# Carrying each token's row number through the experts: scattered results and plain loads in an eight-stage block

## The reference

```
# stage 1: 8 experts, each token goes to the best one, weighted by its probability
x = x + tanh(g_ffn[0]) * p[e*] * (w2[e*] gelu(w1[e*] ln(x) + b1[e*]) + b2[e*])

# stage 3: 8 experts of width 352, each token goes to the best two, beside a shared expert
logits = ln(x) @ gate_w.T ; topk_w, topk_i = top_k(softmax(logits), 2)
eo  = w_down[e] (silu(w_gate[e] ln(x)) * (w_up[e] ln(x)))
out = sum over the two of topk_w * eo  +  sigmoid(ln(x) @ shared_gate_w) * shared(ln(x))
x   = x + tanh(g_ffn[1]) * out
```

## Time and profile before

| | |
|---|---|
| median of three runs | 2610.31 us |
| the profiled execution | 2609.31 us, span 2607.2 us |
| mean granted TensorE clock | 0.933 of full |
| PE busy | 2222.9 us (85%) |
| DVE busy | 1400.3 us (54%) |
| POOL busy | 141.2 us (5%) |
| HBM read and written | 127.49 MB and 29.69 MB |

### The profile page before, as it was taken

The page is one execution under the profiler, slowest core; times in us unless marked ns, Lnnn a source line. Parts: engine busy times, 40 slices in busy tenths (PEclk is TensorE's granted clock), DMA queues, the critical chain, the costliest instruction groups (busy, mean ns, idle before and its releaser), DMA issues. The chain is left out here.

```text
span 2607.2 us, 33940 instructions
## 1 busy us (share of the span) xinstructions
PE 2222.9 (85%) x12885; PEld 1545.4 (59%) x12885; DVE 1400.3 (54%) x2860; ACT 998.1 (38%) x1928; POOL 141.2 (5%) x169
## 2 busy tenths in 40 slices
PE   5896898395999348978579999999999999999988
PEld 3684798143699346854446666666666666665653
DVE  3884110475233157868755555555555555555545
ACT  2221343111111022237634554545445545455435
POOL 0001101101311400000010000000000000000000
PEclk9897899686999679989889999999999999999999
DMA  5101897101399612020000000000000000000000
GB/s 200 55 1 41 277 326 256 41 0 49 105 319 319 203 51 70 1 69 1 10 1 1 1 1 1 1 1 1 1 1 1 1 1 1 1 1 1 1 1 32
DMA packets 105086, 159.37 MB, mean 61 GB/s; under 512 B 12989, under 2 KB 79455, under 8 KB 104927
## 3 DMA queue, kind: packets, MB, share of 16 engines
q1 hardware_dynamic: 95327, 128.36, 14.9%
q0 software_dynamic: 9600, 28.85, 3.1%
HBM read 127.49 MB, written 29.69 MB: 60 GB/s over the span
## 5 line engine op out<-in xcount | busy, mean ns | idle before, releaser
L518 PE MATMUL ps<-arena,w_odd 128*128 128x128 f32 (+4 forms) x2352 | 437.0, 439 | 2.9 <-DVE arena L1691 1.2
L518 PE MATMUL ps<-arena 128*64 128x256 f32 (+6 forms) x2820 | 397.0, 388 | 31.8 <-DVE w_even L1561 7.7
L1981 DVE TENSOR_REDUCE small<-ps 128x1 f32<-128x1024 f32 x256 | 312.6, 1221 | 140.4 <-PE ps L518 140.4
L518 PEld LDWEIGHTS ps<-arena 128*64 128x64 f32 (+5 forms) x2820 | 262.7, 150 | 139.1 <-issue 15.2
L920 PE MATMUL ps<-ident,w_odd 128*128 128x128 f32 x2048 | 295.6, 277 | 24.4 <-ACT arena L1341 22.7
L518 PEld LDWEIGHTS ps<-arena,w_odd 128*128 128x128 f32 (+3 forms) x2352 | 246.7, 188 | 109.5 <-issue 104.2
L1355 ACT ACTIVATE w_odd<-ps,small 128x1101 f32<-128x1101 f32 x256 | 298.9, 1177 | 4.0 <-DVE small L1982 3.5
L920 PEld LDWEIGHTS ps<-ident,w_odd 128*128 128x128 f32 x2048 | 226.6, 141 | 95.0 <-issue 93.2
L1341 ACT ACTIVATE arena<-ps 77x128 f32<-77x128 f32 x256 | 55.8, 268 | 412.6 <-PE ps L927 412.6
L526 PE MATMUL ps<-ident,xn_tok 128*128 128x128 f32 x192 | 33.7, 359 | 191.6 <-DVE xn_tok L1511 191.6
L2000 DVE COPY arena<-ps 128x512 f32<-128x512 f32 x256 | 164.3, 683 | 9.6 <-PE ps L920 8.8
(11 more groups left out here) (333 smaller groups left out, 2949.2 us busy)
## 6 DMA issues: line engine op xcount, KB each, us to landing
w_odd<-in_s_w SPq DMA_DIRECT2D x32, 1024.0 KB, 7.0
w_odd<-in_s_wgu SPq DMA_DIRECT2D x30, 704.0 KB, 6.0
w_even<-in_s_w SPq DMA_DIRECT2D x15, 1024.0 KB, 7.0
arena<-expert_rows_in SPq DMA_DIRECT2D x62, 128.0 KB, 4.9
expert_rows_out<-arena POOLq DMA_DIRECT2D x62, 128.0 KB, 5.1
w_odd<-in_s_wd SPq DMA_DIRECT2D x30, 256.0 KB, 3.8
out_feat<-in_s_wgu SPq DMA_DIRECT2D x10, 704.0 KB, 6.0
expert_rows_in<-zero_row POOLq DMA_DIRECT2D x1, 4992.0 KB, 29.9
```

Source lines behind the costliest of these rows:

```text
L518: return pe.matmul(o, lhsT, rhs, start=start, stop=stop, **kw)
L1981: link(dve.tensor_reduce(m, s6_main[h], AX.X, ALU.max, negate=True))
```

## The change

Rows get four more columns (260 floats, 1040 bytes instead of 1024), and column 256 carries a number: the row of a second DRAM table, `token_rows`, in which the result of this row belongs. The number is 4992 + 128 t + p for token p of tile t, and 2048 more for the token's second choice. DVE makes it once in stage 1, out of a matmul of an upper triangle with a column of ones (which gives p). In stage 3 POOL scatters the 16 tiles of first choices, waits until they have landed, adds 2048 to the numbers (one POOL instruction on 128x16) and scatters the 16 tiles of second choices. An unused row carries 0. DVE takes, for each tile, the larger of the carried number and the row's own place i*128 + p (one instruction on 128x1 a tile); so unused rows go to a spare row each, below 4992. The result of a tile is stored by an indirect DMA to these rows. When all have landed, SP loads the token rows back with plain DMAs of 512 KB, four in stage 1 and eight in stage 3, each group of four token tiles with a semaphore of its own, and DVE combines group by group. The next stage's `bn_stats` move into `combine`, behind each group. SP's row loads wait for DVE's copy (`tx_sb`) instead of the transposes, since DVE now reads the row buffer too. The zero fill waits until stage 0's last context loads have landed (`vo_in`). Semaphores of the weight buffers are shared between the two stages.

```diff
+DX = D + 4
+SPARE = max(SLOTS.values()) * TS
-        XN = sb("xn_tok", [P, NT, D])
+        XNE = sb("xn_tok", [P, NT, DX])
+        XN, row_id = XNE[:, :, 0:D], XNE[:, :, D]
-        ys_dram = {st: nc.dram_tensor(f"expert_rows_out{st}", [SLOTS[st] * TS, D], F32).ap() for st in (1, 3)}
+        yt_dram = {st: nc.dram_tensor(f"token_rows{st}", [SPARE + top * T, D], F32).ap() for st, top in ((1, 1), (3, 2))}
...
 # SP
                 def rows(i):
                     if i >= 2:
-                        sp.wait_ge(per["tx_mm", st], base["tx_mm", st] + i - 1)
+                        sp.wait_ge(per["tx_sb", st], base["tx_sb", st] + i - 1)
...
+            def token_rows(st):
+
+                for q in range(2):
+                    sp.wait_ge(per["ys_out", st, q], base["ys_out", st, q] + 16 * SUB * ((SLOTS[st] + 1 - q) // 2))
+                for g in range(4):
+                    for j in range(1 if st == 1 else 2):
+                        at = SPARE + j * T + 512 * g
+                        dst = (XN if j == 0 else s3_y2)[:, 4 * g:4 * g + 4]
+                        ld(dst, yt_dram[st][at:at + 512].rearrange("(t p) d -> p t d", p=P), yg_in[st][g])
...
                     ld(s4_caus, A["c_caus"], w_in[4])
+                    token_rows(3)
...
 # PE, stage 1
+                mm(PS[:, 6, 0:1], up_tri, ones[:, 0:1]).then_inc(rid_mm, 1)
...
 # POOL
+            pool.wait_ge(vo_in, 64)
             zeroed = [st for st in (1, 3) if st in stages]
...
-                for t in range(NT):
-                    for j in range(top):
-                        pool.indirect_dma_start(xs_dram[st], bass.IndirectOffsetOnAxis(ap=pos_i[:, j, t:t + 1], axis=0), XN[:, t, :], None)\
-                            .then_inc(per["xs_out", st], 16)
+                for j in range(top):
+                    if j == 1:
+                        pool.wait_ge(xs_out[st][0], 16 * NT)
+                        pool.tensor_scalar(row_id, row_id, float(T), None, ALU.add).then_inc(rid_sb, 1)
+                        pool.wait_ge(rid_sb, 2)
+                    for t in range(NT):
+                        pool.indirect_dma_start(xs_dram[st], bass.IndirectOffsetOnAxis(ap=pos_i[:, j, t:t + 1], axis=0), XNE[:, t, :], None)\
+                            .then_inc(xs_out[st][j], 16)
                 for i in range(SLOTS[st]):
                     pool.wait_ge(per["md_sb", st], base["md_sb", st] + SUB * (i + 1))
-                    pool.dma_start(ys_dram[st][i * TS:(i + 1) * TS].rearrange("(j p) d -> p j d", p=P), mx_y[st][i % 2]).then_inc(per["ys_out", st, i % 2], 16)
-                ...
-                        pool.indirect_dma_start(dst, None, ys_dram[st], bass.IndirectOffsetOnAxis(ap=pos_i[:, j, t:t + 1], axis=0))\
-                            .then_inc(per["yg_in", st], 16)
+                    pool.indirect_dma_start(yt_dram[st], bass.IndirectOffsetOnAxis(ap=es_t[:, i:i + 1], axis=0), mx_y[st][i % 2][:, 0], None)\
+                        .then_inc(per["ys_out", st, i % 2], 16)
...
 # DVE
+                dve.tensor_scalar(es_p, es_n, float(TS), row_no, ALU.mult, ALU.add)
...
                     if i + 1 < SLOTS[st]:
                         dve.wait_ge(per["tx_mm", st], base["tx_mm", st] + i + 2)
+                        dve.tensor_scalar(es_t[:, i + 1:i + 2], mx_x[st][(i + 1) % 2][:, 0, D:D + 1], es_p[:, i + 1:i + 2], None, ALU.max)
                         dve.tensor_copy(mx_t[st][(i + 1) % 2].rearrange("p k n -> p (k n)"), PS[:, 6, 0:KD * TS]).then_inc(per["tx_sb", st], 1)
...
             def combine(st, weights):
 
-                dve.wait_ge(per["yg_in", st], base["yg_in", st] + 16 * NT * len(weights))
-                for j, w in enumerate(weights):
-                    for t in range(NT):
-                ...
+                for g in range(4):
+                    dve.wait_ge(yg_in[st][g], 16 * len(weights))
+                    for j, w in enumerate(weights):
+                        for t in range(4 * g, 4 * g + 4):
+                            y = XN[:, t, :] if j == 0 else s3_y2[:, t]
+                            last = dve.scalar_tensor_tensor(out=X[:, t, :], in0=y, scalar=w[:, t:t + 1], in1=X[:, t, :], op0=ALU.mult, op1=ALU.add)
+                        link(last)
+                    for t in range(4 * g, 4 * g + 4):
+                        last = dve.bn_stats(lnst[:, t, :], X[:, t, :])
+                link(last)
...
             def stage2():
-                layer_norm(ln_no[2], tr_no[2])
+                layer_norm(ln_no[2], tr_no[2], stats=False)
...
+            dve.memset(XNE[:, :, D:DX], 0.0)
```

More of the change, by code:

```diff
@@ L140, in build @@
         XO = {1: 4096, 3: 9216}
[L141 removed]
+        mx_x = {st: [cut(AR, XO[st] + 512 * i, SUB, DX) for i in range(2)] for st in (1, 3)}
         mx_t = {st: [cut(AR, XO[st] + 1024 + 512 * i, KD, TS) for i in range(2)] for st in (1, 3)}
@@ L157, in build @@
         es_n = cut(AR, RP + 880 + 10 * NSL, NSL)
+        es_t = cut(AR, RP + 880 + 11 * NSL, NSL).bitcast(U32)
+        rid_p = cut(AR, RP + 880 + 13 * NSL, 1)
+        es_p = cut(AR, RP + 880 + 12 * NSL, NSL)
+        row_no = cut(small, 140, 1)
         s3_y2 = cut(AR, 5120, NT, D)
@@ L298, in build @@
             base[nm, 1], base[nm, 3] = 0, int(v)
-        for nm, each in (("xs_in", 16), ("ys_out", 16)):
+        for nm, each in (("xs_in", 16), ("ys_out", 16 * SUB)):
             for i in range(2):
@@ L302, in build @@
                 base[nm, 1, i], base[nm, 3, i] = 0, each * ((s1n + 1 - i) // 2)
[L303 to L306, removed]
+        for i in range(max(WBUF.values())):
+            turns = (s1n + WBUF[1] - 1 - i) // WBUF[1] if i < WBUF[1] else 0
+            for nm, each in (("w1_in", 32), ("w2_in", 16)):
+                per[nm, 1, i] = per[nm, 3, i] = sem(f"{nm}{i}")
+                base[nm, 1, i], base[nm, 3, i] = 0, each * turns
+        yg_in = {st: [sem(f"yg{st}_in{g}") for g in range(4)] for st in (1, 3)}
+        xs_out = {st: [sem(f"xs{st}_out{j}") for j in range(2)] for st in (1, 3)}
+        zero_out, rid_mm, rid_sb = sem("zero_out"), sem("rid_mm"), sem("rid_sb")
         ends = {s: i + 1 for i, s in enumerate(stages)}
@@ L1498, in link, with layer_norm @@
                 dve.wait_ge(dve_chain, chain[0])
-            def layer_norm(n, tr=None, src=X, gb=None):
-                for t in range(NT):
-                    last = dve.bn_stats(lnst[:, t, :], src[:, t, :])
-                link(last)
+            def layer_norm(n, tr=None, src=X, gb=None, stats=True):
+                if stats:
+                    for t in range(NT):
+                        last = dve.bn_stats(lnst[:, t, :], src[:, t, :])
+                    link(last)
                 for t in range(NT):
@@ L1711, in combine @@
             def combine(st, weights):
-                dve.wait_ge(per["yg_in", st], base["yg_in", st] + 16 * NT * len(weights))
-                for j, w in enumerate(weights):
-                    for t in range(NT):
-                        y = XN[:, t, :] if j == 0 else s3_y2[:, t]
-                        last = dve.scalar_tensor_tensor(out=X[:, t, :], in0=y, scalar=w[:, t:t + 1], in1=X[:, t, :], op0=ALU.mult, op1=ALU.add)
-                    link(last)
+                for g in range(4):
[7 more added lines that the diff above has]
+                        last = dve.bn_stats(lnst[:, t, :], X[:, t, :])
+                link(last)
             def stage1():
```

38 lines of the change are left out of this document (21 added, 17 removed).

## The result

The changed kernel takes 2551.51 us (2548.24 to 2553.83, four runs) where the kernel before takes 2610.36 (2608.93 to 2616.2, four runs): a ratio of 0.9775, with a 95% interval of 0.9756 to 0.9794. The forecast was 2551.0. The profiled execution took 2549.74 us, its span is 2547.9 us (before 2607.2), and the mean granted clock is 0.941 (before 0.933).

The account below looks back on a forecast made before the run. PE was taken as the bound, so gains come only where it stands still. -8.7 + 0.15 - 17.1 - 34.3 + 1 + 0.6 = -58.3 from 2609.3 gave 2551.0 us, range 2539 to 2570.

Parts of the forecast that it names:

- Zero fill at the start: Kernel start: with the fill behind stage 0's context loads, constants land at 11.0 instead of 19.69 us, -8.7 us.
- End of stage 1: Combine after stage 1: plain loads replace 16 gathers and DVE starts at 454.4 instead of 471.89, -17.1 us with links.
- End of stage 3: Combine after stage 3: plain loads in groups let DVE start at 884.5 instead of 919.19, -34.3 us with links.
- load term: End of stage 3: SP's first two loads, 1.05 MB, need 2.7 us of transfer and about 2.3 of issue and landing.
- Even sharing of the engines: Rival at both combines: a group's loads share engines evenly, so DVE waits for all, +4 and +8 us, 2563; chance 0.06.
- Scatter in two halves: Stage 3's start: waiting for the first half and adding to the numbers takes 3.5 us, hidden behind the shared expert, 0.
- Tile loop: Tiles of stages 1 and 3: DVE's extra one-column instruction costs 0 to 0.1 us a tile, taken as +1 us.
- The rival of late row loads: Stage 3's tiles: longer, unaligned rows land 1.3 us later, costing 0.4 us in each of 39 tiles, 2567; chance 0.10.
- Result scatter: Tiles: each result's scatter lands in 5.5 to 6.5 us, within the 7.7 before its buffer is wanted again, 0.
- Small additions: Before the experts: one one-column matmul, three small DVE instructions in stage 1, the es_p row in both stages, +0.6 us.
- The clock: Whole kernel: TensorE's granted clock may return at other moments after shorter pauses, a few us within the main case's 2541 to 2560.
- all cases but the last two: Main case 0.72, late row loads 0.10, even sharing 0.06, no start gain 0.06; excluded: slow scatter 0.03, nothing gained 0.03.

Follow-up runs that it names:

- the late fill alone: Kernel before with one line of the change, the zero fill waiting for stage 0's context loads: 2618.04 us, ratio 0.9969.
- the single wait: Changed kernel, but DVE waits for all four groups of loads before combining the first: 2567.26 us, ratio 0.9783.
- its two variants: Kernel before with only the zero fill delayed, 2618.04 us; kernel before with gathers kept, combine in four groups and statistics in it, 2606.62 us.
- the run with more bytes: Changed kernel with an extra 124 KB transfer ahead of every row load in stages 1 and 3, PE waiting for it too: 2560.69 us.
- the first four runs: Changed kernel with early fill (2568.85 us) or one wait for all groups (2567.26); kernel before with late fill (2618.04) or grouped combine behind gathers (2606.62).

## Why the prediction was right

*Zero fill at the start:* forecast -8.7, traced -8.07 at the first `bn_aggr` and still -8.06 at stage 1's; the late fill alone gave -8.1 us in time by the ratio and -6.6 by the medians, on the other chip. The 11.0 us of the forecast were 11.60, and the loads' packets took 46.0% of the stretch and not the 22.6% of the earlier trace rows, since more of them fell into it. That nothing in stage 0 pays for the fill's new place holds too.

*End of stage 1:* forecast -17.1, traced -16.7. The last scatter landed within 2.4 us of POOL's issue, as the earlier trace rows had it; the first 512 KB came 4.45 us after SP's and not 3.7.

*End of stage 3:* forecast -34.3 (-26 to -36), traced -37.2, just outside its bounds. The load term was right: first group 5.55 us after the issue, forecast 5.8. The mis-sized term is the last scatter, which I had landing 6.4 us after its copy and which SP could pass 3.4 us after it. I took 5.5 us from a crowded stretch; issued at 850.01, it was over by 852.69. It varies: 2.65 to 4.54 us from POOL's issue to SP's in ten traces with that end, 4.27 in one of the unaltered kernel, whose end takes 29.5 us from the last result copy to `bn_aggr` and not 28.1. So of the 2.9 us by which this end beat its forecast, some are the luck of this trace. Even sharing of the engines, a rival, is refuted by the single wait (+13.8).

*Scatter in two halves:* 0, as forecast; the gap was 2.1 us, not 3.5, and hidden.

*Tile loop:* forecast +1 (0 to 4), traced +1.9 from PE's first turn to the last result copy, but that it agrees is chance. I laid it to the instruction ahead of the copy, and that costs nothing: between L1730 copies the distance is 4.18 us in both kernels, and moving the instruction gained nothing. What is longer is six tiles of 4.29 to 4.69 us (the kernel before has four of 4.26 to 4.41), with PE waiting 1.9 us in all for row loads. Two further traces of the same kernel have four such tiles and one. From the first L1730 copy to the last the three take 156.4, 155.5 and 154.7 us; the kernel before takes 155.1 and its two variants, which have rows of 1024 bytes, 155.8 and 156.1, with five such tiles each. So this varies from one execution to the next in both kernels, and no cost of the change can be seen in it. The rival of late row loads did not come about; the run with more bytes shows that 9% more traffic brings it about, at 6 us for stage 3.

*Result scatter:* 5.1 us to landing, forecast 5.5 to 6.5, within the cover of 7.7. Without the overlap it would have cost 34.5 us.

*Small additions:* forecast 0.6; up to stage 1's first scatter 0.7 were lost (-8.06 to -7.35), up to stage 3's 0.4 more, which the shared expert gave back by PE's first turn.

*The clock.* "A few us" were left for the moment at which the granted clock comes back, an estimate for which the prediction had no row, and that is the rest: -2.3 in stage 4 and +3.1 in stage 6, where no instruction changed. The windows say the same; first of the kernel before, then after (granted clock is the third figure from the end, 0.50 being 1.2 GHz and 1.00 2.4 GHz):

```profile
962.00:1002.00 40.00, 30.31 (x155) 22.26 (x151) 23.15 (x37) 11.11 (x27) 0.00 (x0) 0.87 0.56 180
1321.00:1341.00 20.00, 16.48 (x73) 9.90 (x74) 5.52 (x18) 4.58 (x9) 8.82 (x1) 0.91 0.00 0
1341.00:1361.00 20.00, 16.27 (x74) 8.52 (x73) 12.37 (x22) 10.57 (x20) 0.00 (x0) 1.00 0.00 1
```

```profile
902.00:942.00 40.00, 29.60 (x162) 22.09 (x159) 26.91 (x39) 11.76 (x26) 0.00 (x0) 0.96 0.56 180
1258.60:1278.60 20.00, 16.46 (x69) 9.86 (x71) 5.08 (x17) 4.59 (x9) 8.82 (x1) 0.83 0.00 0
1278.60:1298.60 20.00, 16.27 (x66) 7.68 (x63) 10.94 (x19) 9.01 (x16) 0.00 (x0) 0.91 0.00 1
```

Neither can be laid to the change. Stage 4 takes 210.0 and 206.5 us from `bn_aggr` to `bn_aggr` in the two later traces of the unaltered kernel, with a clock of 0.83 and 0.96 at the place of the first window, and 206.2 in the one shown. In stage 6 the trace of the kernel before is the exception: its two variants, which change nothing there, have the 0.83 and 0.91 of the changed kernel in the last two windows, and from the second `bn_aggr` of stage 6 to the end every other trace takes 1299.8 to 1300.3 us, where this one takes 1296.9.

So -8.1, -16.7 and -37.2 are -61.9, less 1.9 up to the end of stage 3's tiles and 0.5 up to that of stage 1's; with -0.8 in stage 2, the clock's -2.3 and +3.1, and the rows of the table that are about nothing, this is the -59.3 of the span. That the total fell within 1 us of the forecast is luck by some 3 us: an end that was better than forecast met a clock that gave less. One slip in the chances: all cases but the last two are 0.94, so "faster by more" could be 0.94 at most, not 0.95.

## What to carry to other kernels

Where a kernel scatters rows, let each row carry the place of its result: the way back is then plain loads, large and in order, and the consumer can start on the first quarter. Count both effects apart; here the loads were worth 40 us, the grouping 14 more. Look at several traces of one kernel before a microsecond or two is laid to a change: here the 1.9 us of the tiles and the 3.1 us of stage 6 were nothing more. Cut such a first group only while the bytes behind it come faster than the consumer uses them.

## What I had not expected of the hardware

*Rows of 1040 bytes.* The zero fill at the same place took 26.3 us with rows of 1024 bytes (one trace) and 31.0 to 34.2 with 1040 (ten traces), at 330 GB/s and at 260 in the slowest, with the engines equally busy. The rule that the prediction weighed, from the Trainium skill, DMA: Bandwidth & Descriptors, How a descriptor splits into AXI transactions, gave an estimate of 13%; the direction agrees, and the size is 1.4 to 2.3 times that. The page words the rule for what a transaction reads, and here it is the rows written to DRAM that begin off the boundary. That misalignment is the mechanism is only argued: an aligned row longer than 1024 bytes was not tried. In the tiles, where 130 KB loads landed in 4.4 us (before 4.7 for 128 KB), nothing of it can be seen.

*A stop of PE, ACT and DVE, left open.* On the chip of the first four runs, both variants of the kernel before lost 12 to 14 us in stage 3's shared expert, while POOL went on issuing its 32 scatters, one every 1.26 us, as on the other chips. PE's timeline in the variant with the late fill:

```profile
662.75 0.59 PE L518 MATMUL ps<-xn_feat,out_feat 128*128 128x512 f32 x1 [1.12 <-issue]
664.16 0.59 PE L518 MATMUL ps<-xn_feat,out_feat 128*128 128x512 f32 x1 [0.82 <-issue]
666.25 0.67 PE L518 MATMUL ps<-xn_feat,out_feat 128*128 128x512 f32 x1 [1.50 <-issue]
669.05 1.01 PE L518 MATMUL ps<-xn_feat,out_feat 128*128 128x512 f32 x1 [2.13 <-issue]
```

Each matmul waits for nothing that the profile shows; the clock fell to 0.50 in it (matmuls of 1.01 us). The size fits the 14 us by which that chip's time for the kernel before is longer, but there is no trace of the kernel before from that chip. Neither variant of the changed kernel that ran there shows it, but whether the pause between the scatter's halves is why was not tried.
